# Cross attention keys loaded into two alternating copies, both units at once, ahead of the queries

## The reference

```python
x = x + self_attention(layernorm(x))                   # causal window of 64 keys
x = x + cross_attention(layernorm(x), ctx, ctx, mask)  # 77 context tokens, mask adds -100
x = x + channel_mix(layernorm(x))                      # sigmoid(r) * (relu(k)**2 @ W_v.T)
```

## Time and profile before

| | |
|---|---|
| runs | 888.1, 896.49, 898.86 us; median 896.49 us |
| profiled execution | span 880.4 us from its first to its last instruction; its time outside the span is not listed apart (median less span: 16.1 us) |
| busy | PE 676.6 us (77%), weight loads 555.9 (63%), DVE 465.6 (53%), ACT 439.7 (50%), POOL 456.8 (52%) |
| TensorE clock | 0.842 granted on the mean |
| DMA | 93.81 MB, 107 GB/s; q1, which SP feeds, has 49.6% of 16 engines |

### The profile page before, as it was taken

How to read it: one execution, slowest core, us unless ns; L and a number is a source line. 1 busy time by engine, 2 the same in 40 slices (tenths; PEclk the granted TensorE clock), 3 DMA queues, 4 the chain that set the end, 5 groups by cost and what they waited for, 6 DMA issues and landing times.

```text
span 880.4 us, 31487 instructions
## 1 busy us (share of the span) xinstructions
PE 676.6 (77%) x13293; PEld 555.9 (63%) x13293; DVE 465.6 (53%) x815; ACT 439.7 (50%) x667; POOL 456.8 (52%) x709
## 2 busy tenths in 40 slices
PE   2357765879778788879688877979898979887683
PEld 2345654667657677668567665868686767665462
DVE  6675353647545456547455454747575656451410
ACT  3042543646546475637455454737574746544230
POOL 7213533255646465755636564565756545644415
PEclk9677887989879799979889798979998989885655
DMA  4753555456545556654656555574757563323000
GB/s 118 98 89 60 104 153 95 139 95 152 96 104 128 108 130 126 140 114 119 96 128 121 106 112 107 139 115 126 129 154 118 133 104 96 101 62 101 10 25 12
DMA packets 86077, 93.81 MB, mean 107 GB/s; under 512 B 16034, under 2 KB 76532, under 8 KB 82868
## 3 DMA queue, kind: packets, MB, share of 16 engines
q1 hardware_dynamic: 85940, 91.81, 49.6%
HBM read 53.32 MB, written 37.40 MB: 103 GB/s over the span
## 4 chain that ended last, share of the span: by engine, by line
PE 44%; DMA 19%; POOL 10%; DVE 8%; issue 8%; SPq 7%; ACT 4%; POOLq 0%; DVEq 0%; ACTq 0%
DMA ck_stack<-ck_scr 14%; PE csums L509 6%; PE proj L302 5%; POOL xn L931 5%; DMA qk_stack<-qk_scr 4%; PE score_exp L494 4%; PE proj L324 4%; SPq L779 4%; PE score_max L368 3%; PE proj L528 3%; PE proj L537 3%; ACT cprobs L1179 2%; PE proj L468 2%; PE sums L433 2%; PE score_max L381 2%
## 5 line engine op out<-in xcount | busy, mean ns | idle before, releaser
L1455 DVE TENSOR_REDUCE cneg_max<-score_max 128x8 f32<-128x616 f32 x128 | 102.0, 797 | 123.4 <-PE score_max L478 123.1
L1179 ACT ACTIVATE cprobs<-score_exp 77x1024 f32<-77x1024 f32 x128 | 129.8, 1014 | 63.3 <-PE score_exp L494 61.7
L931 POOL TENSOR_SCALAR xn<-x,mean,root 128x128 f32<-128x128 f32 x192 | 151.3, 803 | 6.5 <-POOL root L923 6.2
L1455 DVE TENSOR_REDUCE neg_max<-score_max 128x8 f32<-128x1024 f32 (+1 forms) x96 | 117.0, 1219 | 44.2 <-PE score_max L381 27.1
L1179 ACT ACTIVATE probs<-score_exp 128x1024 f32<-128x1024 f32 x96 | 98.0, 1021 | 41.2 <-PE score_exp L399 34.0
L908 POOL TENSOR_TENSOR both<-stats 128x8 f32<-128x8 f32 x48 | 10.2, 212 | 191.1 <-DVE stats L1387 191.1
L478 PE MATMUL score_max<-ck_stack,cq_stack 51*128 51x77 bf16 x1024 | 44.0, 211 | 61.6 <-DMA ck_stack<-ck_scr 58.5
L509 PE MATMUL csums<-cprobs,cv_heads 77*32 77x128 f32 x2048 | 88.2, 303 | 2.5 <-ACT cprobs L1179 2.5
L478 PEld LDWEIGHTS score_max<-ck_stack,cq_stack 51*128 51x128 bf16 x1024 | 27.8, 102 | 76.8 <-DMA ck_stack<-ck_scr 62.6
L302 PE MATMUL proj<-ident,xn 128*128 128x128 f32 x192 | 37.7, 327 | 45.1 <-POOL xn L931 36.7
L494 PE MATMUL score_exp<-cq_stack,ck_stack 53*77 53x128 bf16 x1024 | 60.7, 242 | 11.5 <-ACT cprobs L1179 5.9
(11 more groups left out here) (142 smaller groups left out, 1435.9 us busy)
## 6 DMA issues: line engine op xcount, KB each, us to landing
qk_stack<-qk_scr SPq DMA_DIRECT2D x32, 384.0 KB
cq_stack<-cq_scr SPq DMA_DIRECT2D x64, 192.0 KB, 4.1
qk_stack<-qk_scr SPq DMA_DIRECT2D x32, 256.0 KB
ck_stack<-ck_scr SPq DMA_DIRECT2D x64, 122.7 KB
qk_scr<-q_parts SPq DMA_DIRECT2D x16, 384.0 KB, 2.8
qk_scr<-k_parts SPq DMA_DIRECT2D x16, 384.0 KB, 2.9
cq_scr<-cq_parts SPq DMA_DIRECT2D x16, 384.0 KB, 3.4
x<-in_x_dram SPq DMA_DIRECT2D x16, 256.0 KB, 3.3
```

Of the source, the lines that this page charges most:

```text
L931: nc.gpsimd.tensor_scalar(xn[n][:, b, :], src[:, b, :], mean[n][:, b:b + 1], root[n][:, b:b + 1], ALU.subtract, ALU.mult).then_inc(ln_out[ ...
L1179: nc.scalar.activation(dst, src, ACT.Exp).then_inc(exp_done, 1)
L1455: nc.vector.tensor_reduce(dst, src, AX_X, ALU.max, negate=True).then_inc(max_taken, 1)
```

## The change

The key stack gets two copies, for even and odd quads, and the loads and both matmuls take the copy `q % 2`. So a key load no longer waits for the quad before, but for the one before that. In SP's list `load_ck` of unit 1 moves from behind `load_shift` of unit 1 (step s, quad s-4) to the place right behind `load_ck` of unit 0 (the step before, the same quad), ahead of `load_cq` of unit 0. The ones in the key stack are written for both copies, by the same two memsets of twice the length.

```diff
-        ck_stack = sb("ck_stack", [P, U, I, QB, TC], BF16)
+        ck_stack = sb("ck_stack", [P, 2, U, I, QB, TC], BF16)
...
-                                                ck_stack[r:r + ROWS_BIAS, u, i, b, :], start=True, stop=True)
+                                                ck_stack[r:r + ROWS_BIAS, q % 2, u, i, b, :], start=True, stop=True)
...
-                        last = nc.tensor.matmul(score_exp[0:TC, c:c + T], ck_stack[r:r + ROWS_CROSS, u, i, b, :],
+                        last = nc.tensor.matmul(score_exp[0:TC, c:c + T], ck_stack[r:r + ROWS_CROSS, q % 2, u, i, b, :],
...
+            def load_cross(scr, dst, rows, landed, q, u):
+                for j in range(J):
+                    sp.dma_start(dst[HALF * j:HALF * j + rows, u].rearrange("r i b s -> r (i b s)"),
+                                 scr[q][:, u, j].rearrange("r i s -> r (i s)")).then_inc(landed[u], 16)
+
+            def load_ck(q, u):
+                if q >= 2:
+                    sp.wait_ge(exp_made, max(exp_no[q - 2, u, "c", b] for b in range(QB)))
+                elif q == 0:
+                    sp.wait_ge(cross_rows, 4)
+                    sp.wait_ge(bias_stored, 48)
+                sp.wait_ge(ck_stored, 48 * q + 48)
+                load_cross(ck_scr, ck_stack[:, q % 2], ROWS_BIAS, ck_in, q, u)
+
+            def load_cq(q, u):
                 if q:
                     sp.wait_ge(exp_made, max(exp_no[q - 1, u, "c", b] for b in range(QB)))
                 else:
                     sp.wait_ge(cross_rows, 4)
...
+                sp.wait_ge(cq_stored, 48 * q + 48)
+                load_cross(cq_scr, cq_stack, NROWS, cq_in, q, u)
...
                 if live(s, 2):
                     load_shift(s - 2, 1)
-                if live(s, 4):
-                    load_ck(s - 4, 1)
...
                 if live(s, 3):
                     load_ck(s - 3, 0)
+                    load_ck(s - 3, 1)
                     load_cq(s - 3, 0)
...
-                    nc.vector.memset(ck_stack[rows].rearrange("r u i b t -> r (u i b t)"), 1.0).then_inc(cross_rows, 1)
+                    nc.vector.memset(ck_stack[rows].rearrange("r n u i b t -> r (n u i b t)"), 1.0).then_inc(cross_rows, 1)
```

More of the change, by code:

```diff
@@ L792, in store_cq @@
                 store_cross(cq_parts, cq_scr, RUNS_Q, cq_lo, cq_stored, q)
-            def load_cross(scr, dst, rows, stored, landed, q, u):
+            def load_cross(scr, dst, rows, landed, q, u):
[11 more added lines that the diff above has]
+            def load_cq(q, u):
                 if q:
```

## The result

The changed kernel takes a median of **898.57 us** (897.05 to 901.89, four runs) against 893.91 (888.1 to 898.86) beside it: ratio 1.0135, 95% interval [1.0079, 1.019]. By the medians it is 4.7 us slower, within the 2% that the prediction took for no difference. The forecast was 861 us in a range of 838 to 890, so it was wrong. Executions of one kernel differ here by some 4%; where no interval could be given, the median stands with its lowest and highest.

A forecast was written before the change was run, and what follows sets the result against it. PE was taken to be bound by waits for a unit 1 key load issued late, not by a full DMA system. -58.5 + 19 + 4 = -35.5 us took 896.5 to 861 us, range 838 to 890.

The forecast's parts named there:

- All 14 waits go: -58.5 us.: At PE's first matmuls of a cross maximum, all waits for the unit 1 key load vanish: -58.5 us.
- the 24 that were kept and not taken: Half clock after each removed key wait: up to 24 us could come back; 0 was put in the sum.
- Time taken out of it comes back in full, until another branch of the same circle is later.: On the chain that closes once a quad, removed time is gained in full unless another branch becomes later.
- rival 2: Key wait is moved to the self load and GpSimd; half returns, 29 us stay, 890 us; chance 0.20.
- The queries' delay, 3.3 us.: Two more key loads ahead of the unit 0 queries, at 77 GB/s, make these land 3.3 us later.
- +19 us. This wait is paid in full.: At unit 0's cross maximum PE newly waits 1.9 us for queries in ten of 16 quads: +19 us.
- Rival 1: Queries come late at unit 0's cross maximum, 7.2 us a quad, 115 us added: 957 us; chance 0.10.
- Behind their new place wait the queries of unit 0, the shift rows of unit 0 ...: On SP's list, loads and stores queue behind the moved keys; the move itself adds nothing on SP.
- I take 0, and keep 12.: Next quad's self load may land 0.9 us too late, at most some 12 us over 13 quads; 0 taken.
- Set-up, +4 us.: Key memsets of twice the length on VectorE delay PE in set-up: +4 us, between 0 and 4.2.
- POOL's pause before the moments of x2: Sign on GpSimd: its pause there should shrink from about 4 us to under 2.
- this rule as speaking against the order: On the DMA engines, 51 rows put all four key loads on the same three engines; the sum was left unchanged.

The follow-up runs named there:

- e3: The kernel before, with self loads from the second quad on cut to 128 of 4096 columns of each row: 768.76 us.
- e11: The kernel before, one key copy, key loads at their old places but each cut into 48 and 3 rows: 846.39 us.
- e1: The changed kernel, with the unit 1 keys issued behind the unit 0 queries instead of ahead of them: 869.76 us.
- e5: The changed kernel in its order, with each key load cut into 48 and 3 rows: 853.22 us.
- e7: e5 with the ones of the second key copy written by GpSimd instead of VectorE: 848.46 us.
- e2: The changed kernel's two key copies and longer memsets, with the unit 1 keys issued at their old place: 888.26 us.
- e6: e1 with each self load cut in two, giving descriptors of 4,096 bytes instead of 8,192: 848.42 us.
- e8: e5 with the second copy's ones written by GpSimd and each self load cut in two: 821.87 us.
- e14: The changed kernel with each self load cut in two: 879.6 us.
- e15: The kernel before, one key copy, old places, with key loads cut into 48 and 3 rows and self loads cut in two: 819.95 us.
- e13: The kernel before with each self load cut in two, nothing else: 871.47 us.
- e4: The changed kernel, with self loads from the second quad on cut to 128 of 4096 columns of each row: 834.65 us.
- e9: e1 with self loads from the second quad on cut to 128 of 4096 columns of each row: 803.7 us.
- e12: e4 with two spare float32 matmuls of 512 columns ahead of the first cross maximum of each quad: 821.04 us.
- e10: e5 with self loads from the second quad on cut to 128 of 4096 columns of each row: 777.8 us.

## Why the prediction was wrong, step by step

Two steps failed: the price of the new wait, and that the time of the old one comes back in full. The signs that the prediction named, waits, landing times and memsets, came out nearly as forecast, and the time did not.

- *"All 14 waits go: -58.5 us."* None is left. The half clock behind them gave back 21.7 us more, near the 24 that were kept and not taken. But the premise, that PE waits "for a load that was issued late, not for a full DMA system", was at best half the truth. The load is slow because 51 rows go through few engines beside the self load: with less traffic beside it (e3) the wait is 11.9 us, with 16 engines (e11) none, both at the old place.
- *"Time taken out of it comes back in full, until another branch of the same circle is later."* **The first step that failed.** Pauses of PE took 29.8 us of it and the self load's wait at L368 10.3, and the matmuls in the rest of the quads are 23.8 us slower. Five kernels without the key wait have pauses of 56 to 72 us (the changed one, e1, e5, e7, e11), two with it 36 (before, e2); with halved self loads it is 42 to 49 us in four kernels without it (e6, e8, e14, e15) and 20 in the one with it (e13). So the pauses come with the wait's end, not with the copy or the place. This is rival 2, "the wait is moved, not removed", with about the half that it gave; it looked for it at the self load and GpSimd, and had 0.20.
- *The queries' delay, 3.3 us.* Right in size: they land some 3.9 us later. The 77 GB/s of the earlier trace rows was near the right price, and 1.9 us of wait is what the nine quads have on the mean (17.3 us).
- *"+19 us. This wait is paid in full."* **The second step that failed.** The idle time was right, but 19 was taken for the whole price. The matmuls behind that wait are 20.7 us slower, so it cost 37. In e4 idle time at L478 costs 28.7 us and the slower matmuls 35.9 more. I had counted the half clock as a possible gift of the wait removed, 0 taken and 24 kept, and not at all as a cost of the wait added.
- *Rival 1* had the place of this wait, and a break-even of 3.4 us a quad, reached by 4.8 us of lateness. In the changed kernel the place cost 37 / 16 = 2.3 us a quad, so it alone did not decide. With thin self loads it did: (834.65 - 768.76) / 16 = 4.1 us a quad. Rival 1 was given 0.10, since only its idle time was priced.
- *"Behind their new place wait the queries of unit 0, the shift rows of unit 0 ..."* was costed for the queries alone. With these out of the way the shift rows are late (10.9 us in e1, 20.6 in e9).
- *Self load: "I take 0, and keep 12."* The wait at L368 rose from 14.2 us in 5 waits to 24.5 in 13: near the end that was kept. In e11, with the keys at their old place and no wait for them, it is 19.3 in 11: part of the rise comes with PE's coming earlier, as the prediction had it, and not with the move.
- *Set-up, +4 us.* The first cross maximum is 5.6 us later in the changed kernel (1.1 of it the queries' wait), 3.0 in e5, nothing with the second memset on GpSimd (e7).
- *POOL's pause before the moments of x2* was 4.09 us; at 565.84 us of the changed kernel GpSimd starts them without one, as said. It bought no time: GpSimd now waits longer for the statistics of x1, 7.11 us in that quad.

The account, by the two profiles: forecast -58.5 + 19 + 4 = -35.5, measured +19.3. The new wait cost 18 us more than forecast. The stretch of the old wait came out at -58.5, as forecast, but by luck: 21.7 us of clock came back and as much idle time stayed. The rest of the quad, put at nothing, cost 36. As the profile of before is of a short execution, the 36 is the least certain of these; the stretch of the old wait and the rest together give -22 us, or -16 against e2, instead of -58.5.

By the Trainium skill, "DMA: Bandwidth & Descriptors", section "Why a DMA increments its semaphore by 16 and not by 1", the two pairs of key loads share three engines; e5 agrees, where the same bytes cut into 48 and 3 rows gave 45 us. The prediction named this rule as speaking against the order, and kept a sum in which it cost little.

Open: how the self loads hold PE in its pauses, and why the pauses grow when the key wait goes. Halving the self loads' descriptors gives 19 to 27 us, and with thin self loads no pause reaches 2 us. Nearly all long pauses have an instruction fetch beside them, but that the fetch is what PE waits for was only argued.

## What to carry to other kernels

A load that is waited for may be slow rather than late: look at how many engines move it before moving it ahead, since ahead it delays all that is queued behind it. Price a new wait of TensorE by its idle time and by the clock of the stretch behind it, with the same rows that show what an old wait costs. And before a removed wait is counted in full, look at the waits without a releaser: add them up before and after, as they may grow where the known wait ends. When one step in the line is relieved and the next becomes late (queries, then shift rows), the thing to change is the load itself.

## What the runs showed of the hardware that was not expected

- Idle times of PE of 1.62 and 2.83 us were followed by stretches at a mean of 0.63 and at 0.50 of the clock, the latter for 8.69 us without a gap in PE's work. Over 16 quads, 40.6 us of such waits went with 38.2 us of slower matmuls behind them (e4 against e3). Two spare matmuls a quad in the place of the wait made those matmuls as fast as without it, and gained 14 us (e12).
- PE's pauses without a releaser were 36 us where PE waited for the keys (before, e2) and 56 to 72 us where it did not (e1, e5, e7, e11 and the changed kernel); with thin self loads they were 2.5 to 5.2 us (e3, e4, e9, e10, e12).
- Key loads of 51 rows cost 45 to 48 us more than 48 and 3 rows (898.57 to 853.22; 894.08 to 846.39), though the bytes are the same.
- Self loads cut from descriptors of 8,192 bytes to 4,096 gained 19 to 27 us in each of five kernels (before to e13, the changed one to e14, e1 to e6, e7 to e8, e11 to e15; all but the first compared across two times of measuring), though their bytes are the same and their DMAs twice as many.
